# Row normalisation moved from ScalarE to GpSimd, in a fused MLP, attention, MLP kernel on one Trainium2 core

## What is computed

```python
x = x + 0.5 * ffn(_layernorm(x), w_gate, w_up, w_down)
x = x + attn(_layernorm(x), Wq, Wk, Wv, Wproj, lq1, lk1, lq2, lk2)
x = x + 0.5 * ffn(_layernorm(x), w_gate, w_up, w_down)

def _layernorm(x, axis=-1, eps=1e-05):
    m = jnp.mean(x, axis=axis, keepdims=True)
    v = jnp.var(x, axis=axis, keepdims=True)
    return (x - m) / jnp.sqrt(v + eps)
```

## Time and profile before

| | |
|---|---|
| median of 3 runs | 2110.51 us (2108.02 to 2113.64) |
| the profiled execution: its own time | 2114.67 us |
| its span, first to last instruction | 2112.9 us |
| busy, share of the span: PE | 1863.1 us, 88% |
| ACT | 1706.1 us, 81% |
| DVE | 1550.5 us, 73% |
| POOL | 1374.2 us, 65% |
| granted clock of TensorE, mean | 0.983 |

### The profile page before, as it was taken

The page is one execution under the profiler, slowest core; times in us unless marked ns, Lnnn a source line. Parts: engine busy times, 40 slices in busy tenths (PEclk is TensorE's granted clock), DMA queues, the critical chain, the costliest instruction groups (busy, mean ns, idle before and its releaser), DMA issues. The chain is left out here.

```text
span 2112.9 us, 39423 instructions
## 1 busy us (share of the span) xinstructions
PE 1863.1 (88%) x13634; PEld 784.6 (37%) x13634; DVE 1550.5 (73%) x3324; ACT 1706.1 (81%) x2531; POOL 1374.2 (65%) x1439
## 2 busy tenths in 40 slices
PE   2677999999998999999999898999999888999866
PEld 1243443343433434344432443444433333432223
DVE  7889988686747898777955988888866678741375
ACT  3455988979888898878989888888889889889952
POOL 8788886666645786677853876876854657640155
PEclk9899999999999999999999999999999999999998
DMA  4134454234222445243331445343341344220013
GB/s 127 31 67 81 84 85 75 58 68 79 43 48 45 74 75 103 56 78 59 73 64 21 80 78 91 69 83 54 58 93 32 58 81 81 60 49 1 11 34 72
DMA packets 477493, 136.16 MB, mean 64 GB/s; under 512 B 458224, under 2 KB 477040, under 8 KB 477296
## 3 DMA queue, kind: packets, MB, share of 16 engines
q1 hardware_dynamic: 477296, 133.65, 34.4%
HBM read 11.96 MB, written 8.39 MB: 10 GB/s over the span
## 5 line engine op out<-in xcount | busy, mean ns | idle before, releaser
L1061 ACT ACTIVATE probs<-psum 128x1024 f32<-128x1024 f32 (+3 forms) x1280 | 1069.5, 934 | 80.5 <-PE psum L1346 64.1
L1364 PE MATMUL psum_o<-probs,v_sb 128*32 128x512 f32 (+3 forms) x5120 | 569.3, 540 | 16.7 <-POOL probs L967 10.6
L1309 PE MATMUL psum<-w_gu_T,xT 128*128 128x512 f16 (+1 forms) x2304 | 504.5, 367 | 49.4 <-DVE hq L1143 14.3
L1346 PE MATMUL psum<-q_stack,k_stack 64*128 64x512 f16 (+3 forms) x2560 | 384.8, 352 | 81.8 <-ACT probs L1061 62.4
L1309 PEld LDWEIGHTS psum<-w_gu_T,xT 128*128 128x128 f16 x2304 | 213.7, 99 | 314.0 <-issue 48.2
L967 POOL TENSOR_SCALAR_AFFINE_SELECT probs<-probs 128x512 f32<-128x512 f32 x256 | 179.4, 707 | 204.7 <-ACT probs L1061 203.8
L1322 PE MATMUL psum<-w_down_T,hT 128*128 128x256 f16 x2176 | 265.9, 278 | 34.4 <-DMA hT<-h 21.4
L1346 PEld LDWEIGHTS psum<-q_stack,k_stack 64*128 64x128 f16 x2560 | 99.6, 93 | 494.7 <-ACT probs L1061 385.3
L934 POOL TENSOR_TENSOR hq<-grid,qscale 128x704 f32<-128x704 f32 x128 | 183.7, 1437 | 100.5 <-DVE grid L1160 100.5
L1322 PEld LDWEIGHTS psum<-w_down_T,hT 128*128 128x128 f16 x2176 | 209.6, 99 | 97.2 <-issue 30.3
L941 POOL TENSOR_TENSOR h<-hq,h 128x704 f16<-128x704 f32 x128 | 202.3, 1580 | 65.4 <-ACT h L1017 64.7
(11 more groups left out here) (120 smaller groups left out, 2355.1 us busy)
## 6 DMA issues: line engine op xcount, KB each, us to landing
xb<-L_attn_x SPq DMA_DIRECT2D x16, 512.0 KB, 4.1
out<-xb SPq DMA_DIRECT2D x16, 512.0 KB, 3.4
xT<-x SPq DMA_TRANSPOSE x128, 3.1
hT<-h SPq DMA_TRANSPOSE x128, 3.5
k_stack<-st SPq DMA_TRANSPOSE x64, 3.2
q_stack<-st SPq DMA_TRANSPOSE x64, 3.3
k_stack<-L_ffn_w_down SPq DMA_DIRECT2D x1, 704.0 KB, 4.1
k_stack<-L_ffn_w_gate SPq DMA_DIRECT2D x1, 512.0 KB, 5.3
```

What stands on the lines that cost most here:

```text
L1061: nc.scalar.activation(probs[:, s % 3, 2 * u:2 * u + 2, q0:CHUNK], psum[:, plan.pairs[s, u]:plan.pairs[s, u] + 2, q0:CHUNK], ACT.Exp, scal ...
L1309: last = nc.tensor.matmul(bank(e)[:, 0:hi - lo], xs[:, x, t % 2, k, :], w_gu_T[:, w, k, lo:hi], start=n == 0, stop=n == len(parts) - 1)
L1346: last = nc.tensor.matmul(psum[:, plan.pairs[s, u] + j, q0:CHUNK], k_stack[half, at, h, kt % NTC * P:(kt % NTC + 1) * P], q_stack[half, c ...
L1364: last = nc.tensor.matmul(psum_o[at:at + VD, q0:CHUNK], v_sb[:, kt // NTC % SLOTS * NTC + kt % NTC, 2 * g + u, :], probs[:, s % 3, 2 * u + ...
```

## The change

- `norm_a` leaves ACT and becomes a POOL stage of two TENSOR_SCALAR instructions of 128x256 per pair. Each subtracts the mean and multiplies by the root, both read per partition.
- `rstd` loses the two instructions that made `offset`, and its last multiplication now signals the end: six instructions in place of eight.
- In the set-up, `norm_a` of chunk 0 goes to POOL, behind `rstd` and ahead of the third `scaled_weights`.
- A pair of pass 1 now always names the pair before it as a need, also at the first pair of a chunk.
- The planner's costs and delays are set for this, and 99 rows of `DUE` (all) and the four of `WIDE` have new numbers, so every engine's order changes.

```diff
-    "norm_a1": (-2323132, 491991, -41621, 891713, -68036, 1081174, 443696, 757181, -56983, 1833622, 602430, 565892, 814835, 1828334, -1240848, -601801, 2717350, 2248735, 1496559, 3404069, 5855075, 6048472, -406357, 704529, 2460362, 3825428, 1682135, 2138170, 4002539, 3788248, 231101, 861625),
+    "norm_a1": (-2437185, 1310960, 128790, 795297, -243377, 1252325, 997309, 1284221, 923275, 2609238, 1200061, 766441, 476263, 1541088, -1181082, 30622, 2579699, 1826955, 658570, 2970510, 6365666, 6972148, 138260, 1608974, 2386074, 2826460, 1819761, 2101749, 4360539, 4504470, 192420, 1163451),
...
-WIDE = {0: (1, 2, 3, 5, 6, 7, 10, 13, 14, 15), 1: (1, 2, 3, 4, 5, 6, 8, 11, 13, 14, 15), 2: (0, 2, 3, 5, 7, 9, 11, 12, 13, 14, 15), 3: (1, 2, 3, 4, 6, 7, 9, 10, 11, 13, 15)}
+WIDE = {0: (1, 2, 4, 5, 12, 13, 14, 15), 1: (0, 1, 2, 3, 4, 7, 10, 11, 14, 15), 2: (1, 2, 3, 4, 6, 7, 8, 9, 10, 11, 12, 13, 14, 15), 3: (2, 3, 4, 5, 6, 7, 9, 10, 11, 12, 14, 15)}
...
-            add(norm, "scalar", at("norm_a"), needs, takes, frees)
+            add(norm, "gpsimd", at("norm_a"), needs, takes, frees)
...
-                add(norm, "scalar", of_pair("norm_a", *pair), [("rstd", 1, c), ("norm_a", "x", 1, pair[1] - 1) if i else None,
+                add(norm, "gpsimd", of_pair("norm_a", *pair), [("rstd", 1, c), ("norm_a", "x", 1, pair[1] - 1) if t else None,
...
-                    n, o = EARLY_RSTD[e], offset[:, slot, :]
-                    nc.gpsimd.tensor_scalar(o, mean_var[:, slot, :, 0], -1.0, None, ALU.mult)\
-                        .then_inc(mean_negated, 1)
-                    nc.gpsimd.tensor_tensor(rstd[:, slot, :], t, y, ALU.mult).then_inc(early_rstd, 1)
-                    pool.wait_ge(mean_negated, n + 1)
-                    pool.wait_ge(early_rstd, n + 1)
-                    nc.gpsimd.tensor_tensor(o, o, rstd[:, slot, :], ALU.mult).then_inc(rstd_ready, 1)
+                    nc.gpsimd.tensor_tensor(rstd[:, slot, :], t, y, ALU.mult).then_inc(rstd_ready, 1)
+                elif e[0] == "norm_a":
...
+                    pool.wait_ge(rstd_ready, RSTD["rstd", pas, 2 * p // NTC] + 1)
+                    for j in range(2):
+                        t = 2 * p + j
+                        i = t % NTC
+                        last = nc.gpsimd.tensor_scalar(a[:, j * C:(j + 1) * C], xb[:, t % XB, :],
+                                                       mean_var[:, slot, i, 0:1], rstd[:, slot, i:i + 1],
+                                                       ALU.subtract, ALU.mult)
+                    last.then_inc(early_normed, 1)
...
-                    act.wait_ge(rstd_ready, RSTD["rstd", pas, 2 * p // NTC] + 1)
-                    for j in range(2):
-                        t = 2 * p + j
-                        i = t % NTC
-                        last = nc.scalar.activation(a[:, j * C:(j + 1) * C], xb[:, t % XB, :], ACT.Identity,
-                                                    bias=offset[:, slot, i:i + 1], scale=rstd[:, slot, i:i + 1])
-                    last.then_inc(early_normed, 1)
...
-                    gpsimd_stages(pool, first["rstd"])
+                    gpsimd_stages(pool, first["rstd"] + first["norm_a"])
...
-                        if i == 2:
-                            scalar_stages(act, first["norm_a"])
```

More of the change, by code:

```diff
@@ L147 @@
[L147 removed]
[8 rows of a table removed]
+    "add_down0": (-2597887, -1045783, -3697192, -2832321, 106648, 354990, 372209, 1968117, 3018988, 4603412, -1176545, -378672, -325724, 518453, -2106456, 1566182, -404941, -340737, 2410961, 3215403, 1451323, 2678617, 4329316, 4350124, 1752434, 1857079, 1645548, 3807498, -239447, 2100689, 1302775, 3845202),
@@ new lines @@
+    "high_qk": (-2516242, -674472, -1923895, -653306, -519109, -11134, -1511568, 1470019, 3107857, 5174565, 871005, 990281, 3587372, 3896817, 1882687, 2942232, 2247462, 5016585, 1247095, 2822637, 4463674, 5642769, 1069182, 3369247, 4438840, 4125761, 2628757, 4630083, 2220338, 2683696, -1823439, -1268204),
[4 rows of a table added]
+    "load": (122595, 122595, 151687, 151687, -249324, -249324, 126250, 126250, -10280, -10280, 1214106, 1214106, -422261, -422261, 502469, 502469, -872380, -872380, 1136526, 1136526, -138467, -138467, 879971, 879971, 369476, 369476, 1766810, 1766810, 238853, 238853, 2938610, 2938610),
@@ L195 @@
 DRAIN = 170
-LATE = {("rstd", "norm_a"): 55, ("high_qk", "low_qk"): 60, ("copy_o", "transpose_o"): 85, ("scores", "exp"): 60}
+LATE = {("high_qk", "low_qk"): 60, ("copy_o", "transpose_o"): 85, ("scores", "exp"): 60}
 AFTER = {("grid_h", "points_h"): 35, ("grid_x", "points_x"): 35, ("gate", "gate"): 100, ("gate", "quant_h"): 100,
          ("add_out", "stats"): 90, ("add_down", "stats"): 90, ("head_sum", "head_stats"): 90,
-         ("head_stats", "norm_heads"): 35, ("rope", "rms"): 35, ("store", "load"): 50, ("norm_a", "scale_x"): 35}
+         ("head_stats", "norm_heads"): 35, ("rope", "rms"): 35, ("store", "load"): 50, ("rstd", "norm_a"): 90}
 EARLY = dict(quant_h=460, scale_x=390)
@@ L204 @@
 PORT = dict(grid_h=0, points_h=0, norm_qk=0, norm_heads=0, divide_x=0, dequant_x=0, low_x=0, divide_h=0,
-            dequant_h=0, low_h=0, rope_add=0, low_qk=0, mask=0)
+            dequant_h=0, low_h=0, rope_add=0, low_qk=0, mask=0, norm_a=0)
 PORT_LEAD = 140
@@ L743, in macaron_kernel @@
         QUANT = ordinals(order["vector"], ("quant_h", "scale_x"))
-        EARLY_NORM = ordinals(order["scalar"], ("norm_a",))
-        EARLY_RSTD = ordinals(order["gpsimd"], ("rstd",))
+        EARLY_NORM = ordinals(order["gpsimd"], ("norm_a",))
         DIVIDE = ordinals(order["gpsimd"], ("divide_x", "divide_h"))
@@ L920, in gpsimd_stages @@
                     pool.wait_ge(root_steps, n + 5)
-                    n, o = EARLY_RSTD[e], offset[:, slot, :]
-                    nc.gpsimd.tensor_scalar(o, mean_var[:, slot, :, 0], -1.0, None, ALU.mult)\
-                        .then_inc(mean_negated, 1)
-                    nc.gpsimd.tensor_tensor(rstd[:, slot, :], t, y, ALU.mult).then_inc(early_rstd, 1)
-                    pool.wait_ge(mean_negated, n + 1)
-                    pool.wait_ge(early_rstd, n + 1)
-                    nc.gpsimd.tensor_tensor(o, o, rstd[:, slot, :], ALU.mult).then_inc(rstd_ready, 1)
+                    nc.gpsimd.tensor_tensor(rstd[:, slot, :], t, y, ALU.mult).then_inc(rstd_ready, 1)
+                elif e[0] == "norm_a":
+                    pas, p = e[2:]
+                    slot = STAT[pas, 2 * p // NTC] % STATS
+                    a = buffers("x", (pas, p))[0]
+                    before = last_low("x", (pas, p))
+                    if before:
+                        pool.wait_ge(low_ready, before)
+                    pool.wait_ge(rstd_ready, RSTD["rstd", pas, 2 * p // NTC] + 1)
[6 more added lines that the diff above has]
+                    last.then_inc(early_normed, 1)
                 elif e[0] in ("dequant_x", "dequant_h"):
```

73 lines of the change are left out of this document (30 added, 43 removed), and 134 rows, old and new, of the table DUE.

## The result

The changed kernel takes 2215.8 us (median of 4 runs, 2209.61 to 2216.07) against 2110.94 us for the kernel before in the same comparison (2108.02 to 2113.64). The ratio is 1.0487, with a 95% interval of 1.0469 to 1.0505: 4.9% slower. The forecast was 2092, with a range that ended at 2116.

What follows compares the result with a forecast made beforehand. PE and ACT were both taken as near their limit, PE late more often. ACT's freed time -22.9, port +1, lead +2, tail +1.2 gave -18.7 us, from a median of 2110.5 to 2092; range 2060 to 2116.

Steps and rivals of the forecast that it cites:

- What POOL gets: Whole run: each moved instruction takes 0.43 us on POOL, 192 of them 83 us (44 to 119); POOL no bound.
- What ACT is spared: Middle, first to last `exp`: 80 pairs at 0.98 us take 78.4 us off ACT, its load falling from 87% to about 83%.
- PE's idle time for `exp`: Sign in the middle: PE's idle time waiting for `exp` should fall from 62 us to under 45.
- ACT's idle time for PE: Sign in the middle: ACT's idle time waiting for PE should rise from 151 us to over 190.
- a sign of being wrong: Prediction counts as wrong if, among other signs, ACT's waits for PE grow by as much as its work shrinks.
- The share of 0.29: Middle: part of ACT's freed 78.4 us that shortens the run, from waits 62.4 / (62.4 + 151.5); gain 22.9 us.
- my sum: Whole run: gain from ACT less costs of port, lead and tail, -22.9 + 1 + 2 + 1.2 = -18.7 us.
- The order: Whole run: the refitted order can win or lose a little; put in the range, not in the sum.
- The lead and the tail: Before the first and after the last `exp`: 2 us (0 to 8.4) and 1.2 us (-1 to 3) longer.
- The port: Port shared by POOL and DVE: more POOL work adds waits, booked at 1 us (0 to 4).
- the 5% I named: Sign on DVE: the two-input instructions on hidden tiles should keep their mean times within 5%.
- POOL holds up the chain of an MLP tile: Rival: normalisation queues ahead of POOL's steps on MLP tiles; run grows by 13.6 us, to 2124; chance 17%.

Runs made afterwards that it cites:

- run 3: Changed kernel, same order, moved instruction subtracting constant 0 and multiplying by constant 1, so rows are copied, not normalised: 2172.4 us, ratio 1.0295.
- run 5: Changed kernel, same order, with an AFFINE_SELECT that copies rows in place of the normalising instruction: 2082.0 us, ratio 0.9857.
- run 9: Changed kernel's order with six forms of the POOL instruction at 32 places each, for their durations, rows not normalised: one execution, 2121.2 us.
- run 10: Changed kernel, same order, with one multiplication by the root and the mean not subtracted: 2151.9 us, ratio 1.019.
- run 11: Changed kernel's order with six pairs of operations in the POOL instruction, for their durations, rows not normalised: one execution, 2113.4 us.
- run 12: Changed kernel, same order, mean negated by an extra small instruction, then add and mult for subtract and mult: 2113.9 us, ratio 0.9999.
- run 8: Kernel before, only the normalising steps moved to POOL, as row-copying AFFINE_SELECT, every other step in its old order: 2132.2 us, ratio 1.0091.
- run 7: Kernel before, only the normalising steps moved to POOL with the changed kernel's instructions, every other step in its old order: 2287.8 us, ratio 1.0829.
- run 1: Kernel before, normalisation still on ACT, with the changed kernel's DUE and WIDE tables: 2264.1 us, ratio 1.0721.
- run 2: Changed kernel with the DUE and WIDE tables of the kernel before: 2315.4 us, ratio 1.097.
- run 4: Changed kernel with the planner's price of a normalised pair at 2440 ns in place of 830, tables kept: 2240.6 us, ratio 1.0606.
- run 6: Kernel before with the planner's price of ACT's pair at 830 in place of 1090, tables and instructions kept: 2215.9 us, ratio 1.0487.
- run 13: Changed kernel's order, pair copied by AFFINE_SELECT and signalled at once, then seven small POOL instructions nobody waits for: 2260.3 us, ratio 1.0715.

## Why the prediction was wrong, step by step

**What POOL gets: the step that failed.** I took the price of the new instruction from rows of other operations by their size, "On a straight line between 230 at 4 and 637 at 512", 0.43 us, with a two-input operation, 0.618, as upper bound. It took 1.22 us, twice the bound, and 248 us in all where I had 83 (44 to 119). The straight line was sound for what it was made from: a copy of this size by the masks' operation takes 0.40. The error was to treat the arithmetic as free and the choice of operations as immaterial. Runs 3, 5 and 9 to 12 show that this choice sets the length, and with `add` in place of `subtract` (run 12) 102 of the 105 us are gone.

Same order, from short to long (run 12 has one small instruction more per root):

| run | instruction | median us | POOL busy us | time us |
|---|---|---|---|---|
| 5 | copy by select | 0.40 | 1438.4 | 2082.0 |
| 12 | add, mult | 0.56 | 1488.7 | 2113.9 |
| 10 | mult | 0.93 | 1537.3 | 2151.9 |
| 3 | subtract, mult, constants | 1.07 | 1561.1 | 2172.4 |
| changed kernel | subtract, mult | 1.22 | 1585.6 | 2215.8 |

Counted from run 5, runs 12, 10 and 3 cost 0.63, 0.71 and 0.74 us of run per us of POOL work, and the changed kernel 0.91. At 72% of the span POOL is no bound by its share, yet most of each added microsecond reaches the end. The last step is the steepest, 43 us of run for 24.5 us of POOL. PE's busy time, 1868 to 1875 us in the first four rows, is 1900 us in the changed kernel, and the mean granted clock of the profiled execution falls from 0.977 (run 3) to 0.963. So part of this step is PE at a lower clock; its share of the 43 us was not measured.

**What ACT is spared, and how much of it counts.** ACT's busy time fell by 82 us, not 104 (to 1623.6; run 5 has 1620.1, so it isn't an effect of the slowdown). The profile accounts for the rest. Summed by groups of instructions, ACT's spans fell by 115 us, from 1861.9 to 1747.1: 105.4 of normalisation and 9 of small changes in the others. But neighbouring spans overlap, and the busy time counts an overlap once: 155.8 us before, 123.5 now. By my own price of 0.98 us a pair it should have been 94. "PE's idle time for `exp`" rose to 74.8 instead of falling under 45. Even in run 5, with a cheap instruction, it was 52.3. ACT's idle time for PE rose by 60 us to 99.5 + 78.3 + 17.8 + 16.0 = 211.6, over the 190 forecast, but that is nearly as much as its work in the middle shrank (63), which I had named as a sign of being wrong. In run 5 the direction is the one I meant: 79.0 + 78.4 + 21.3 + 11.3 = 190.0, 38.5 more than before against 66.5 us less work. The share of 0.29 was not shown: in run 5 the middle is 1794 us, 23 less than before, which looks like my 22.9; but run 8, the move alone with the same cheap instruction, is 19 us *slower* than before, where my sum had it 19 faster, and only the refitted order makes it 31 faster. So even with the price met the sum was off by some 38 us for the move alone. That run 5, at 2082, lies inside my range is luck: two terms that I had missed, of opposite signs.

**The order: booked at 0.** It was worth 50 to 72 us (runs 7 and 8 against run 5 and the changed kernel). To book it "in the range and not in the sum" was wrong: runs 1, 2, 4 and 6 show steps of 25 to 152 us by tables and prices alone.

**The lead and the tail.** I had 12.0 us of POOL for the lead's 28 instructions; they took 39.78, POOL was busy 188.8 of 211 us and the first `exp` came 6 us later. In the tail four took 4.84 and not 1.7. Lead and tail grew by 15 us, not 3. With the cheap instruction (run 5) the first `exp` came 8 us earlier than before, but the tail is 97 us there too, 6 more than before. So most of the tail's growth is not the long instruction. What it shows in both kernels is a lower granted clock, 0.76 and 0.75 in place of 0.88, and 64 us of PE's work in place of 58.

**The port.** The two-input DVE instructions that I named took 148.3 + 150.3 us before and 158.8 + 143.5 now:

```profile
L1146 DVE SCALAR_TENSOR_TENSOR hq<-grid,hq 128x704 f32<-128x704 f32 x128 | 158.8, 1241 | 58.1 <-ACT grid L995 57.7
L1151 DVE SCALAR_TENSOR_TENSOR grid<-grid,hq 128x704 f32<-128x704 f32 x128 | 143.5, 1122 | 0.7
```

Their sum grew by 3.7 us although POOL worked 211 us more. It does not follow POOL's work in the other runs of this order either: 302.8 us in run 5, 290.6 in run 3, 302.3 in the changed kernel. So my reading that all their time above the shortest goes to waits for POOL is not borne out. On POOL's side, the moved instruction takes 1.30 us in the mean beside a median of 1.22, some 15 us over 192. The port was the right thing to weigh against the change and looks small here; what it costs the run, booked at 1 us, was not isolated. The first had a mean 6.9% above that of before, over the 5% I named, the second 4.7% below.

**The rival.** "POOL holds up the chain of an MLP tile" is what happened, with its place right (ACT's steps on hidden tiles wait for POOL) and its price not: 13.6 us, worked out with the same 0.43. The price of the longer instruction is the 134 us between run 5 and the changed kernel, which run 13 gives too by its rate (0.85 x 158 us). It is a measured price: nothing in the trace of the kernel before gives this rate. Its chance of 17% was too small for the one case that hung on a price which no row showed.

## What to carry to other kernels

An operation whose exact form (operation pair, kind of operand) no row of the trace has is not bounded by rows of the same size: measure that form by itself before moving work, since here one word of it, `add` for `subtract`, decided between no change and 4.9% slower. On an engine that many chains cross, count how long a step holds the queue, and not only when its own result is due: at 69 to 72% busy POOL still passed on 0.6 to 0.9 of every added microsecond. Where an order is fitted to a list of costs, a move and its refit are one change; here either half alone, and even a corrected price without a refit, was slower.

## What the runs showed of the hardware

POOL's TENSOR_SCALAR on 128x256 fp32 took 0.41 us with two of `add` and `mult` and constants, 0.55 to 0.56 with per-partition values, 0.86 and 0.93 with one `mult`, 0.94 with one `subtract`, and 1.07 to 1.23 with `subtract` and `mult` in either order. A single `mult` costs more than a pair of them. A copy took 0.40 and a two-input multiply 0.61. The Trainium skill (GPSIMD Engine Reference, Engine selection) calls one-input elementwise work on this engine "roughly line-rate". What that rate is no run here shows; the traces show that no single rate holds, as forms of the same shape took from 0.40 to 1.23 us. Why `subtract` and a lone operation are slow was not tried.

TensorE's granted clock had a mean of 0.98 of full speed in the middle of the changed kernel (PE busy 91%), where it was 1.00 before (93%), and of 0.75 in the tail, where it was 0.88. What brought it down there was not tried.
